# Layer norm and gate logits computed tile by tile inside the attention and neighbour loops

## The chip, the cores and the metric

The kernel runs on one core of one Trainium2 chip. The metric is the device time of one execution in microseconds (us), and for a kernel the median of its runs.

## What is computed

A graph network with a mixture of experts, in two layers: masked attention over 3327 nodes of 256 features, experts, a neighbour sum, experts again. Each stage takes the layer norm of the running x and adds its result to x. Cut from the reference:

```python
def _layernorm(x, axis=-1, eps=1e-05):
    m = jnp.mean(x, axis=axis, keepdims=True)
    v = jnp.var(x, axis=axis, keepdims=True)
    return (x - m) / jnp.sqrt(v + eps)
# attention (L0_gnn): h = x @ edge_w; e = where(adj > 0, h @ h.T, NEG_BIG)
#   output = adj * (node_att * softmax(e, axis=1)) @ (x @ weight) + bias
# experts (both ffn): logits = xt @ Wg + bg   (the second has no bias)
#   top_vals, top_idx = top_k(logits, 2); top_probs = softmax(top_vals)
#   y = sum over the 8 experts of gate * expert(xt)
# neighbours (L1_gnn): relu((adj @ x) @ W.T + b)
x = x + _L0_gnn_ref(_layernorm(x), adj, ...)
x = x + _L0_ffn_ref(_layernorm(x)[None], L0_ffn_Wg, L0_ffn_bg, ...)[0]
x = x + _L1_gnn_ref(_layernorm(x), adj, L1_gnn_W, L1_gnn_b)
x = x + _L1_ffn_ref(_layernorm(x)[None], L1_ffn_gate_w, ...)[0]
```

The change concerns the second and the fourth layer norm, and the logits `xt @ Wg` that follow them.

## The kernel before

Rows of x are handled in 26 tiles of 128 (T = 26, the last with 127). The program is a series of stages with a barrier of all engines between them: `project`, `attend`, `route` and `experts` of layer 0, `combine`, `neighbours`, `route` and `experts` of layer 1, `combine`. Inside a stage each engine runs its own instruction list in order, with waits on semaphores; nothing reorders them. `tiles` (L42) unrolls the first two and the last two tiles of a loop and runs the rest two at a time, with two buffer slots.

- **attend.** GpSimd copies the tile's h (L399) and turns its adjacency row block into a mask (L401). TensorE computes the scores of tile t+1 in 7 chunks (L502), then multiplies the probabilities of tile t in 7 groups of up to 4 blocks (L537, L539). VectorE masks the scores of t+1 (L444), forms the low parts of the transposed probabilities group by group (`rest`, L429), and then writes x_out (L471 to L478) and its row sums (`bn_stats`, L482). SP loads the adjacency (L371) and x, and stores x_out (L359). The row sums of all tiles stay in one buffer, `ST`.
- **route.** VectorE turns `ST` into mean and 1/std for all tiles (L133 to L146, with the square root on ScalarE, L151), SP loads all of x again (L690), VectorE normalises it tile by tile (L791), TensorE transposes it (L733) and multiplies it by the gate weights (L747) with copies on ScalarE (L778), SP stores the normalised x to `xn` in DRAM (L697) for the experts' gathers, and loads the expert weights (L928, L929). From L813 on the routing chain follows, nearly all on VectorE: top two, softmax, places of the pairs.
- **neighbours.** For tile t TensorE transposes the stored mask in 4 groups (L1326), ScalarE (L1384) and VectorE (`odd`, L1417) widen them, TensorE multiplies by the normalised x (L1333). The tail of tile t-1 stands inside tile t: `add` on VectorE (L1423), two transposes (L1342), the product with W (L1348), and `finish` on VectorE: pre (L1427), x_out (L1433), row sums (L1436). GpSimd makes two identities and then has nothing to do. SP loads the mask two tiles ahead (L1298), stores x_out (L1293) and loads x (L1301).

VectorE's step of the neighbour loop, before:

```python
def step(t, uses, slot, first, last):
    very_first = first and slot == 0
    if not very_first:
        add(t - 1, 1 - slot, first)
    odd(t, slot, 1, first)
    odd(t, slot, 3, first)
    if not very_first:
        finish(t - 1, uses - (1 - slot), 1 - slot, first)
```

## Time and profile before

| | |
|---|---|
| median of 3 runs | 1936.64 us (1935.55 to 1937.98) |
| span of the profiled execution | 1937.9 us, 1.3 us above the median |
| TensorE busy | 1616.8 us (83%) |
| VectorE busy | 995.0 us (51%) |
| ScalarE busy | 663.5 us (34%) |
| GpSimd busy | 480.1 us (25%) |

The stages begin at about 88 us (attention), 652 (gate 0), 734 (experts 0), 1066 (combine), 1127 (neighbours), 1368 (gate 1), 1448 (experts 1) and 1892 (last combine). In the profile PE is TensorE's matmuls, PEld its weight loads, DVE VectorE, ACT ScalarE, POOL GpSimd, SP the queue that issues most transfers; a q behind the name is the engine's queue of DMA issues. The text behind `<-` at the end of a row is what ended the idle time before it.

### The profile page before, as it was taken

Reading aid. Unit: us, or ns where it says so; the run is one execution under the profiler, and the core shown is the slowest. Engines: PE = TensorE matmul, PEld = TensorE weight load, DVE = VectorE, ACT = ScalarE, POOL = GpSimd, SP = SyncE. Lnnn points to the kernel's source line nnn. Section 1 sums busy time; section 2 is a strip of 40 time slices with the busy share of each in tenths; the row PEclk is TensorE's granted clock in tenths of the full one; section 3 lists DMA queues with packets and bytes.
Section 4 is the critical chain, followed back from the end, with each engine's and each line's share of the span. In section 5 each row is a group of like instructions: output and inputs, shape, how many; then the busy total and the mean of one; then the engine's idle time right before and its main releaser. Section 6 shows DMA issues by size and latency. Waiting matters only on the chain. (4 is left out here: it accounts for less than half of the span.)

```text
span 1937.9 us, 34014 instructions
## 1 busy us (share of the span) xinstructions
PE 1616.8 (83%) x9896; PEld 1358.5 (70%) x9896; DVE 995.0 (51%) x2459; ACT 663.5 (34%) x1395; POOL 480.1 (25%) x812
## 2 busy tenths in 40 slices
PE   5899999999999647999998059999729999999990
PEld 4788888888888635778777035555617888888880
DVE  5455555555555464555553632323385556566543
ACT  2323333333333202223222523333204454554554
POOL 0021121121111004555554000000013454544530
PEclk9999999999999757999999579999559999999995
DMA  4033433433432551111111824333751111111118
GB/s 152 8 112 137 154 116 132 149 126 116 146 145 81 191 234 33 46 50 50 49 49 43 282 90 138 122 131 120 292 227 31 35 38 35 36 36 37 36 32 284
DMA packets 84823, 209.45 MB, mean 108 GB/s; under 512 B 8880, under 2 KB 66225, under 8 KB 80561
## 3 DMA queue, kind: packets, MB, share of 16 engines
q1 hardware_dynamic: 68176, 154.95, 23.0%
q0 software_dynamic: 11328, 30.95, 5.1%
q10 hardware_dynamic: 5280, 23.09, 3.0%
q8 instruction: 17, 0.28, 0.1%
q14 instruction: 22, 0.18, 0.0%
HBM read 150.89 MB, written 58.07 MB: 108 GB/s over the span
## 5 line engine op out<-in xcount | busy, mean ns | idle before, releaser
L1062 PE MATMUL bank<-ffn_w_in_parts,ffn_x_t 128*128 128x512 f32 x1416 | 363.6, 404 | 18.9 <-DVE ffn_w_in_parts L1189 18.8
L1062 PEld LDWEIGHTS bank<-ffn_w_in_parts,ffn_x_t 128*128 128x128 f32 x1416 | 259.4, 191 | 78.6 <-DVE ffn_w_in_parts L1189 28.1
L1086 PE MATMUL bank<-ffn_w_out_parts,ffn_hidden_t 128*128 128x256 f32 x2124 | 286.0, 289 | 25.8 <-DVE ffn_hidden_t L1178 25.7
L1086 PEld LDWEIGHTS bank<-ffn_w_out_parts,ffn_hidden_t 128*128 128x128 f32 x2124 | 264.5, 193 | 30.3 <-issue 20.0
L502 PE MATMUL bank<-h_t,attn_h_tile 128*128 128x512 f32 (+1 forms) x1092 | 250.7, 385 | 10.5 <-POOL attn_h_tile L399 6.8
L537 PE MATMUL bank<-support,attn_probs_t 128*128 128x512 f32 x650 | 245.4, 411 | 1.1 <-DVE attn_probs_t L429 1.1
L502 PEld LDWEIGHTS bank<-h_t,attn_h_tile 128*128 128x128 f32 x1092 | 199.3, 192 | 51.9 <-POOL attn_identity L389 7.0
L417 ACT CAST attn_probs_t<-bank 128x512 fp32r<-128x512 f32 (+1 forms) x182 | 98.8, 558 | 350.0 <-PE bank L511 350.0
L1128 ACT ACTIVATE ffn_silu_or_gelu<-bank,w_b_in 128x128 f32<-128x128 f32 x472 | 134.2, 367 | 190.6 <-PE bank L1073 190.6
L429 DVE TENSOR_TENSOR attn_probs_t<-bank,attn_probs_t 128x512 fp32r<-128x512 f32 (+1 forms) x182 | 116.5, 652 | 161.4 <-ACT attn_probs_t L417 161.4
L539 PE MATMUL bank<-support,attn_probs_t 128*128 128x256 f32 x676 | 185.6, 281 | 0.0
L1333 PE MATMUL bank<-normed_parts,nbr_adj_t 128*128 128x512 f16 x676 | 165.1, 383 | 7.7 <-ACT nbr_adj_t L1384 7.7
L444 DVE CUSTOM_DVE_ANT_0 attn_scores<-bank,attn_mask 128x512 f32<-128x512 f32 (+1 forms) x182 | 116.5, 648 | 66.4 <-issue 66.4
L1178 DVE TENSOR_TENSOR ffn_hidden_t<-ffn_silu_or_gelu,ffn_hidden_t 128x512 fp32r<-128x512 f32 x118 | 80.5, 692 | 133.4 <-ACT ffn_hidden_t L1134 133.4
L537 PEld LDWEIGHTS bank<-support,attn_probs_t 128*128 128x128 f32 x650 | 122.3, 188 | 23.5 <-issue 1.3
L1025 POOL DMA_INDIRECT y<-ffn_y,ffn_dst x118 | 122.5, 1038 | 56.1 <-issue 55.9
L1014 POOL DMA_INDIRECT ffn_x_gathered<-xn,ffn_tok x118 | 126.9, 1075 | 20.5 <-issue 5.3
L539 PEld LDWEIGHTS bank<-support,attn_probs_t 128*128 128x128 f32 x676 | 127.6, 189 | 1.1
L399 POOL CAST attn_h_tile<-h_t 128x512 fp32r (+1 forms) x26 | 15.9, 611 | 416.2 <-DMA adj_tile<-in_adj 416.1
L1326 PE MATMUL bank<-nbr_identity,nbr_mask 128*128 128x128 bf16 x676 | 56.0, 222 | 73.5 <-DMA nbr_mask<-mask 71.9
L1326 PEld LDWEIGHTS bank<-nbr_identity,nbr_mask 128*128 128x128 bf16 x676 | 47.4, 99 | 90.5 <-issue 72.6
L1333 PEld LDWEIGHTS bank<-normed_parts,nbr_adj_t 128*128 128x128 f16 x676 | 61.4, 99 | 68.4 <-ACT nbr_adj_t L1384 12.0
(233 smaller groups left out, 2221.9 us busy)
## 6 DMA issues: line engine op xcount, KB each, us to landing
adj_tile<-in_adj SPq DMA_DIRECT2D x25, 1663.5 KB, 8.5
mask<-attn_mask ACTq DMA_DIRECT2D x26, 832.0 KB, 3.4
nbr_mask<-mask SPq DMA_DIRECT2D x26, 832.0 KB, 4.4
comb_y<-y SPq DMA_DIRECT2D x12, 768.0 KB, 10.4
w_w_in<-in_w SPq DMA_DIRECT2D x2, 4096.0 KB, 17.7
w_w_in<-in_w_t SPq DMA_DIRECT2D x2, 4096.0 KB, 17.4
x_normed<-x SPq DMA_DIRECT2D x6, 768.0 KB, 7.1
xn<-x_normed SPq DMA_DIRECT2D x6, 768.0 KB, 35.3
```

The lines of the kernel that those rows point to most:

```text
L429: dve.tensor_tensor(PT[:, half(slot, g), 1, 0:gn * P], bank[4 + half(slot, g)][:, 0:gn * P], PT[:, half(slot, g), 0, 0:gn * P].bitcast(F32 ...
L444: dve.tensor_tensor_reduce(out=SC[:, slot, c0:c0 + cn], in0=bank[c % 4][:, 0:cn], in1=NEG[:, slot, c0:c0 + cn], scale=1.0, scalar=-3.0e38, ...
L502: ins = pe.matmul(bank[c % 4][:, 0:cn], HS[:, slot, hs, k, :], HT[:, hm, k, c0:c0 + cn], start=n == 0 and k == 0, stop=n == 2 and k == KD - 1)
L537: pe.matmul(bank[6 + slot][:, :], part[:, 0, :], SUP[:, jt, :, :].rearrange("p a d -> p (a d)"), start=jt == 0, stop=False)
L539: ins = pe.matmul(bank[6 + slot][:, 0:D], part[:, 1, :], SUP[:, jt, 0, :], start=False, stop=False)
L1014: pool.indirect_dma_start(out=XG[:, slot, :], out_offset=None, in_=a["xn"], in_offset=bass.IndirectOffsetOnAxis(ap=TOKS[:, slot:slot + 1], ...
L1025: pool.indirect_dma_start(out=a["y"], out_offset=bass.IndirectOffsetOnAxis(ap=DSTS[:, slot:slot + 1], axis=0), in_=YS[:, slot, :], in_offs ...
L1062: ins = pe.matmul(bank[2 + 2 * slot + b][:, :], XT[:, slot, xp, k, :], WIP[:, wp, k, b * CH:(b + 1) * CH], start=n == 0 and k == 0, stop=n ...
L1086: ins = pe.matmul(bank[7][:, 0:D], HTT[:, hp, k, :], WOP[:, wp, k, :], start=n == 0 and k == 0, stop=n == 2 and k == KH - 1)
L1128: ins = act.activation(GATE[:, j, k * P:(k + 1) * P], src[:, k * P:(k + 1) * P], ACT.Gelu, bias=w.BI[:, bass.ds(e * KH + (4 * j + k), 1)])
L1326: ins = pe.transpose(bf[g % 2][:, j * P:(j + 1) * P], NEG[:, slot, (g0 + j) * P:(g0 + j + 1) * P], ID[:])
L1333: ins = pe.matmul(bank[2 + slot][:, :], AT[:, g % 2, j * P:(j + 1) * P], XH[:, g0 + j, :, :].rearrange("p a d -> p (a d)"), start=g0 + j = ...
```

## The change

A class `Gate` does layer norm and logits of one row tile inside the loop that produces the tile. VectorE aggregates the tile's own row sums (`stats`), GpSimd computes 1/std by a power and one Newton step in 8 dependent operations of one column, normalises the tile into `XN`, and multiplies it by all 8 gate vectors at once (`norm`, a product of 128 x 2048); SP stores `XN`; VectorE sums the products in four pieces of two experts (`reduce`) and adds the bias (`logits`). In attention GpSimd runs `norm(t - 3)` at the head of its step t, and VectorE sums tile t-1 between the groups of tile t. In the neighbour loop GpSimd runs `norm` alone, and VectorE sums tile t-2 in step t. At the start of each loop stage GpSimd waits for the gate weights, broadcast to 128 partitions, and reorders them.

The gate stages keep only the routing chain. The weights of layer 0 are loaded at the start of gate 0; `w_in` of layer 1 is loaded in step 3 of the neighbour loop's SP queue, `w_out` and the biases in gate 1.

```diff
+class Gate:
+    NORM_STEPS = 8
+    PIECES = 4
...
+    def load(self, act):
+        flat = self.gate_w.rearrange("p k e -> (p k e)")
+        act.dma_start(self.PR[:].rearrange("p e d -> p (e d)"), flat.partition_broadcast(P)).then_inc(self.w_loaded, 16)
...
+    def prepare(self, pool):
...
+        pool.wait_ge(self.w_loaded, 16 if self.gate_b is None else 32)
+        raw = self.PR[:].rearrange("p e d -> p (e d)").rearrange("p (q k e) -> p e k q", k=KD, e=E)
+        for k in range(KD):
+            pool.tensor_copy(self.GW[:, :, k * P:(k + 1) * P], raw[:, :, k, :]).then_inc(self.w_ready, 1)
+        pool.wait_ge(self.w_ready, self.n_ready())
...
+    def stats(self, dve, t, slot):
+        dve.bn_stats(self.ROW[:, slot, :], self.XO[:, slot, :]).then_inc(self.sums_ready, 1)
+        dve.wait_ge(self.sums_ready, t + 1)
+        if not known(t) or t >= 2:
+            dve.wait_ge(self.normed, t - 1)
+        dve.memset(self.TAKER[:], 0.0)
+        dve.bn_aggr(self.MV[:, slot, :], self.ROW[:, slot, :]).then_inc(self.stats_ready, 1)
+
+    def norm(self, pool, t, uses, slot):
+        def link(ins):
+            ins.then_inc(self.norm_step, 1)
+            link.n += 1
+            pool.wait_ge(self.norm_step, t * self.NORM_STEPS + link.n)
...
+        pool.wait_ge(self.stats_ready, t + 1)
+        link(pool.tensor_tensor(v, var, eps, ALU.add))
+        link(pool.tensor_tensor(minus, mean, minus_one, ALU.mult))
+        link(pool.tensor_tensor(r, v, minus_half, ALU.pow))
+        link(pool.tensor_tensor(tmp, r, r, ALU.mult))
+        link(pool.tensor_tensor(tmp, tmp, v, ALU.mult))
+        link(pool.tensor_tensor(tmp, tmp, minus_half, ALU.mult))
+        link(pool.tensor_tensor(tmp, tmp, three_halves, ALU.add))
+        link(pool.tensor_tensor(r, r, tmp, ALU.mult))
+        if not known(t) or t >= 2:
+            pool.wait_ge(self.xn_stored[slot], uses * 16)
+        pool.tensor_tensor(self.POOL_TAKER[:], eps, eps, ALU.add)
+        pool.tensor_scalar(self.XN[:, slot, :], self.XO[:, slot, :], minus, r, ALU.add, ALU.mult).then_inc(self.normed, 1)
+        pool.wait_ge(self.normed, t + 1)
+        if not known(t) or t >= 1:
+            pool.wait_ge(self.reduced, t * self.PIECES)
+        pool.tensor_tensor(self.PR[:], self.XN[:, slot, :].unsqueeze(1).to_broadcast([P, E, D]), self.GW[:],
+                           ALU.mult).then_inc(self.product_ready, 1)
+
+    def store(self, sp, t, slot):
+        sp.wait_ge(self.normed, t + 1)
+        sp.dma_start(self.xn[bass.ds(t * P, P), :], self.XN[:, slot, :]).then_inc(self.xn_stored[slot], 16)
+
+    def reduce(self, dve, t, slot, piece):
+        n = E // self.PIECES
+        dve.wait_ge(self.product_ready, t + 1)
+        dve.tensor_reduce(out=self.LS[:, slot, piece * n:(piece + 1) * n], in_=self.PR[:, piece * n:(piece + 1) * n, :],
+                          axis=AX, op=ALU.add).then_inc(self.reduced, 1)
+
+    def logits(self, dve, t, slot):
...
+        dve.wait_ge(self.reduced, (t + 1) * self.PIECES)
+        dve.tensor_tensor(self.LG[:, t, :], self.LS[:, slot, :], self.GB[:], ALU.add).then_inc(self.logits_ready, 1)
...
@@ attend, gpsimd
                 def step(t, uses, slot, first, last):
+                    if not known(t) or t >= 3:
+                        gate.norm(pool, t - 3, uses - 2 + slot, 1 - slot)
                     if not first:
                         pool.wait_ge(adj_in[slot], uses * 16 + (16 if last else 0))
...
                 pool.wait_ge(edge, 1)
-                tiles(pool, T, step)
+                gate.prepare(pool)
+                tiles(pool, T, step, head=6)
+                for t in range(T - 3, T):
+                    gate.norm(pool, t, t // 2, t % 2)
@@ attend, vector
-                    rest(t, slot, range(EARLY, NG))
+                    for g in range(EARLY, NG):
+                        rest(t, slot, [g])
+                        if g - EARLY < Gate.PIECES and not (first and slot == 0):
+                            gate.reduce(dve, t - 1, 1 - slot, g - EARLY)
+                    if not (first and slot == 0):
+                        gate.logits(dve, t - 1, 1 - slot)
...
-                    dve.bn_stats(a["ST"][:, t, :], XO[:, slot, :]).then_inc(sums_ready, 1)
+                    gate.stats(dve, t, slot)
...
+                for piece in range(Gate.PIECES):
+                    gate.reduce(dve, T - 1, (T - 1) % 2, piece)
+                gate.logits(dve, T - 1, (T - 1) % 2)
@@ route, sync
-                for sem, (lo, hi) in zip(x_loaded, spans):
-                    sp.dma_start(X[:, lo:hi, :], view[:, lo:hi, :]).then_inc(sem, 16)
-
-                sp.wait_ge(x_loaded[-1], 16)
-                w.load(sp)
...
-                    sp.dma_start(out[:, lo:hi, :], X[:, lo:hi, :]).then_inc(xn_stored, 16)
-                sp.wait_ge(xn_stored, len(spans) * 16)
+                load(sp)
...
@@ neighbours, sync
                     sp.dma_start(NEG[:, slot, :], a["mask"][t, :, :]).then_inc(mask_in[slot], 16)
+                    if not known(t) or t >= 3:
+                        gate.store(sp, t - 3, 1 - slot)
                     if not first:
                         store(t - 2, slot)
                     sp.dma_start(XB[:, slot, :], a["x2"][bass.ds(t * P, P), :]).then_inc(x_loaded[slot], 16)
-                tiles(sp, T, step)
...
+                    if known(t) and t == 3:
+                        w.load_in(sp)
+                tiles(sp, T, step, head=4)
@@ neighbours, gpsimd
+                gate.prepare(pool)
+                tiles(pool, T, lambda t, uses, slot, first, last: gate.norm(pool, t, uses, slot))
@@ neighbours, vector
-                    dve.bn_stats(a["ST"][:, t, :], XO[:, slot, :]).then_inc(sums_ready, 1)
+                    gate.stats(dve, t, slot)
...
                     odd(t, slot, 1, first)
+                    if not first:
+                        for piece in range(Gate.PIECES // 2):
+                            gate.reduce(dve, t - 2, slot, piece)
                     odd(t, slot, 3, first)
+                    if not first:
+                        for piece in range(Gate.PIECES // 2, Gate.PIECES):
+                            gate.reduce(dve, t - 2, slot, piece)
+                        gate.logits(dve, t - 2, slot)
                     if not very_first:
                         finish(t - 1, uses - (1 - slot), 1 - slot, first)
...
                 tiles(dve, T, step)
+                for t in (T - 2, T - 1):
+                    for piece in range(Gate.PIECES):
+                        gate.reduce(dve, t, t % 2, piece)
+                    gate.logits(dve, t, t % 2)
```

The transposes and the 8-column matmuls of `route`, its square root and its normalisation leave the program; the normalised x of all tiles is no longer kept in SBUF.

Where the moved work stands on VectorE in the neighbour loop is the point on which most depends. One tile of its list (an unrolled one, t = 24), before; `nbr_sum` is `add`, `nbr_adj_t` is `odd` for groups 1 and 3, the last three rows are `finish` of tile 23:

```order
L1423 TENSOR_TENSOR nbr_sum<-bank,nbr_sum_hi 128x256
L1417 TENSOR_SCALAR nbr_adj_t<-bank 128x1024
L1417 TENSOR_SCALAR nbr_adj_t<-bank 128x256
L1427 TENSOR_TENSOR nbr_before_relu<-bank,nbr_bias 128x256
L1433 SCALAR_TENSOR_TENSOR nbr_x_out<-nbr_before_relu,nbr_x 128x256
L1436 BN_STATS row_sums<-nbr_x_out 128x6
```

The same tile of VectorE's list in the changed kernel, where the sums are those of tile 22 and the statistics those of tile 23:

```order
L1489 TENSOR_TENSOR nbr_sum<-bank,nbr_sum_hi 128x256
L1483 TENSOR_SCALAR nbr_adj_t<-bank 128x1024
L240 TENSOR_REDUCE nbr_logit_sums<-nbr_gate_products 128x2 x2
L1483 TENSOR_SCALAR nbr_adj_t<-bank 128x256
L240 TENSOR_REDUCE nbr_logit_sums<-nbr_gate_products 128x2 x2
L247 TENSOR_TENSOR logits<-nbr_logit_sums,nbr_gate_b 128x8
L1493 TENSOR_TENSOR nbr_before_relu<-bank,nbr_bias 128x256
L1499 SCALAR_TENSOR_TENSOR nbr_x_out<-nbr_before_relu,nbr_x 128x256
L198 BN_STATS nbr_row_sums<-nbr_x_out 128x6
L202 MEMSET nbr_dve_wait_taker 128x1
L203 BN_AGGR nbr_mean_var<-nbr_row_sums 128x2
```

Four sums and the logits of the tile before stand ahead of `finish`, two of them ahead of the second widening.

GpSimd's list at the start of the attention stage, in the changed kernel:

```order
L492 MEMSET attn_identity 128x128
L494 AFFINE_SELECT attn_identity<-attn_identity 128x128
L496 MEMSET adj_tile 128x2
L184 MEMSET attn_constants 128x1 x4
L190 COPY attn_gate_w<-attn_gate_products 128x8x128 x2
L505 CAST attn_h_tile<-h_t 128x512
L507 ISA
L507 TENSOR_SCALAR attn_mask<-adj_tile 128x3328
```

The constants and the two reordering copies are new there, and stand ahead of the first tile's copy and mask.

## Rows read from the trace of the kernel before

**Rows 1.** Windows: two stages; busy us (instructions) by engine, clock, DMA share, GB/s
```profile
core 0: us, PE busy (x) PEld busy (x) DVE busy (x) ACT busy (x) POOL busy (x), PEclk, DMA share, GB/s
88.00:652.00 564.00, 552.71 (x3120) 478.56 (x3120) 295.39 (x962) 181.10 (x234) 93.30 (x55) 0.99 0.35 124
...
1127.00:1368.00 241.00, 221.03 (x1508) 132.13 (x1508) 67.33 (x156) 69.85 (x104) 0.93 (x4) 0.96 0.37 122
```
**Rows 2.** Timeline, gate 0: start, us, engine, line, operation [idle before, releaser]
```profile
651.96 4.06 SPq L690 DMA_DIRECT2D x_normed<-x  x4
...
654.20 0.13 POOL L724 IOTA gate_pair_low<- 128x1 f32 x1
...
693.49 0.37 DVE L813 TENSOR_REDUCE gate_top<-gate_logits 128x26 f32<-128x208 f32 x1
```
**Rows 3.** Timeline, gate 1: its start and the chain's first reduction
```profile
1368.14 3.70 SPq L690 DMA_DIRECT2D x_normed<-x  x4
...
1407.21 0.37 DVE L813 TENSOR_REDUCE gate_top<-gate_logits 128x26 f32<-128x208 f32 x1
```
**Rows 4.** DMA issues, 652 to 735 us: KB each, median us to landing
```profile
w_w_out<-in_w SPq DMA_DIRECT2D x1, 4096.0 KB, 33.3
...
xn<-x_normed SPq DMA_DIRECT2D x3, 768.0 KB, 34.5
```
**Rows 5.** Timeline, experts 0, GpSimd: two dependent operations of one column
```profile
803.85 0.20 POOL L1010 COPY ffn_tok<-route_tok 128x1 int32 x1
804.13 0.19 POOL L1013 TENSOR_TENSOR ffn_wait_taker<-ffn_identity 128x1 f32<-128x1 f32 x1
```
**Rows 6.** Groups by shape, GpSimd: the mask; busy us, mean ns
```profile
L401 POOL TENSOR_SCALAR attn_mask<-adj_tile 128x3328 bf16<-128x3328 f32 x26 | 77.1, 2964 | 9.3 <-issue 7.3
```
**Rows 7.** Timeline, attention, about one tile: VectorE and GpSimd
```profile
318.65 0.43 DVE L482 BATCH_NORM_STATS2 row_sums<-attn_x_out 128x256 f32 x1
...
326.77 0.61 POOL L399 CAST attn_h_tile<-h_t 128x512 fp32r x1 [17.15 <-DMA adj_tile<-in_adj]
...
329.85 0.69 DVE L429 TENSOR_TENSOR attn_probs_t<-bank,attn_probs_t 128x512 fp32r<-128x512 f32 x1 [1.58 <-ACT attn_probs_t L417]
331.69 0.69 DVE L429 TENSOR_TENSOR attn_probs_t<-bank,attn_probs_t 128x512 fp32r<-128x512 f32 x1 [1.15 <-ACT attn_probs_t L417]
```
**Rows 8.** Timeline, gate 0, VectorE: a sum over 472 elements
```profile
704.72 0.65 DVE L860 TENSOR_REDUCE gate_value<-gate_expert_cmp 128x59 f32<-128x472 f32 x1
```
**Rows 9.** Timeline, attention start: the first mask, and who waits for it
```profile
96.31 2.96 POOL L401 TENSOR_SCALAR attn_mask<-adj_tile 128x3328 bf16<-128x3328 f32 x1 [7.32 <-issue]
...
99.39 0.06 DVE L443 MEMSET attn_wait_taker<- 128x1 f32 x1 [12.84 <-POOL attn_mask L401]
...
100.19 4.21 PE L502 MATMUL bank<-h_t,attn_h_tile 128*128 128x512 f32 x9 [3.65 <-DVE attn_max L444]
```
**Rows 10.** DMA issues: a small broadcast and a large load, us to landing
```profile
adj_tile<-in_adj SPq DMA_DIRECT2D x25, 1663.5 KB, 8.5
...
attn_bias<-in_bias SPq DMA_DIRECT2D x1, 128.0 KB, 3.3
```
**Rows 11.** Timeline, attention end: the last tile's statistics
```profile
649.19 0.43 DVE L482 BATCH_NORM_STATS2 row_sums<-attn_x_out 128x6 f32<-128x256 f32 x1
```
**Rows 12.** Timeline, neighbour loop, one tile of VectorE
```profile
1342.49 0.42 DVE L1427 TENSOR_TENSOR nbr_before_relu<-bank,nbr_bias 128x256 f32<-128x256 f32 x1 [2.30 <-PE bank L1348]
...
1343.62 0.43 DVE L1436 BATCH_NORM_STATS2 row_sums<-nbr_x_out 128x256 f32 x1
...
1348.53 0.29 DVE L1417 TENSOR_SCALAR nbr_adj_t<-bank 128x256 f16<-128x256 bf16 x1 [3.25 <-PE bank L1326]
...
1351.05 0.42 DVE L1427 TENSOR_TENSOR nbr_before_relu<-bank,nbr_bias 128x256 f32<-128x256 f32 x1 [2.23 <-PE bank L1348]
```
**Rows 13.** Timeline, neighbour end: the last but one tile's statistics
```profile
1360.62 0.43 DVE L1436 BATCH_NORM_STATS2 row_sums<-nbr_x_out 128x6 f32<-128x256 f32 x1
```
**Rows 14.** Windows, attention start, behind TensorE's wait: columns as in rows 1
```profile
100.20:104.20 4.00, 4.00 (x9) 3.13 (x10) 2.49 (x11) 0.00 (x0) 2.78 (x1) 0.50 1.04 366
```

More of the change, by code:

```diff
@@ L39, with tiles @@
 PAIR_ROWS = 2 * NP
-def tiles(eng, count, step):
+def tiles(eng, count, step, head=2):
     turns = (count - 2) // 2
-    step(0, 0, 0, True, False)
-    step(1, 0, 1, True, False)
-    with eng.Fori(1, turns) as i:
+    for t in range(head):
+        step(t, t // 2, t % 2, t < 2, False)
+    with eng.Fori(head // 2, turns) as i:
         step(i * 2, i, 0, False, False)
@@ L1301, in step @@
                     sp.dma_start(XB[:, slot, :], a["x2"][bass.ds(t * P, P), :]).then_inc(x_loaded[slot], 16)
-                tiles(sp, T, step)
-                store(T - 2, 0)
-                store(T - 1, 1)
+                    if known(t) and t == 3:
+                        w.load_in(sp)
+                tiles(sp, T, step, head=4)
+                gate.store(sp, T - 3, (T - 3) % 2)
+                for t in (T - 2, T - 1):
+                    store(t, t % 2)
+                    gate.store(sp, t, t % 2)
+                gate.end(sp)
                 for slot in range(2):
@@ L1376, in _ @@
                 act.dma_start(BB[:], a["b"].partition_broadcast(P)).then_inc(w_loaded, 16)
+                gate.load(act)
                 def even(t, slot, g, first):
```

172 lines of the change are left out of this document (78 added, 94 removed).

## The prediction

> **What bounds the kernel now.** I read the stages first, by windows. In the attention stage TensorE is busy 552.7 of 564 us, in the neighbour stage 221.0 of 241 us [rows 1]: both loops run at TensorE's pace, VectorE is half busy or less, and GpSimd does nearly nothing in the neighbour stage (0.93 us). Then the timeline of the two gate stages. Gate 0 starts at 651.96 and the first reduction of its routing chain at 693.49 [rows 2]; gate 1 starts at 1368.14 and its chain at 1407.21 [rows 3]. That head, 41.5 and 39.1 us, is normalising, transposing and multiplying all 26 tiles, and nothing else runs beside it but transfers. It is what the change moves into the loops. So the question is whether the loops carry it for nothing. I took one tile of each loop and asked when the moved work can begin, and who waits for its result.
>
> **The heads go: -76.5 us.** What stays ahead of the chain is GpSimd's constants: its last one begins at 654.20 and takes 0.13 us, 2.4 us into the stage [rows 2]; without the two identity instructions it ends some 2.0 us in. So gate 0 gains 41.5 - 2.0 = 39.5 and gate 1 39.1 - 2.1 = 37.0. The weights of layer 0 are now loaded at the start of gate 0, beside a chain of 42 us: 12 MB landed within 34 us of their issue [rows 4], so I cost this at nothing; if that load were slower by 10 us, the experts would wait for it.
>
> **GpSimd's price for one tile, L.** L runs from the end of VectorE's row statistics to the finished product. Eight dependent 128x1 operations come first, each waiting for the one before: such a pair stands 0.28 us apart [rows 5], so 8 x 0.28 = 2.25. Then the wait taker 0.19, and the norm of 256 elements. The one-input rate of GpSimd is (2.96 - 0.19) / 3328 = 0.83 ns an element [rows 5, 6], so 0.19 + 0.21 = 0.40. Then a wait, 0.12, and the product: 2048 elements of two inputs. No row shows a large two-input operation on GpSimd. Bounds from the mask row: one pass over the elements, 0.19 + 1.7 = 1.9; two reads and a write with no overlap, three passes, 5.3. I take two and a half passes, 4.45, since an engine that needs a full pass for one input will hardly take the second free, and some of the write may overlap. With 0.2 for the two hand-overs between engines, **L = 7.6 us** (5.05 to 8.5). The power operation could cost more than 0.28; no row shows it, and I allow 1 us on top for it.
>
> The Trainium skill (GPSIMD Engine Reference, section 3.1) speaks against putting this product here: it gives 4497 ns for a GpSimd add of two fp32 inputs of 2048 elements, about twice VectorE. By that figure the sum below would be the same; by the one-pass price it would be 69 us lower. No trace so far shows which holds.
>
> **Attention loop: 0.** A tile takes 21.1 us. Statistics end at 319.1 [rows 7]; with the new aggregate (0.3, an estimate from VectorE's small operations of 0.15 to 0.2) L ends at 327.0. The first sum stands behind the group's subtraction that starts at 329.85, so after 330.5: 3.5 us to spare. A sum reads 512 elements, 0.65 x 512 / 472 = 0.70 us [rows 8], and stands in a gap of 1.15 us that VectorE has before each subtraction. GpSimd's next tile copy waits for the adjacency until 326.77, so the norm ahead of it delays the mask by 0.2 us, and TensorE wants that tile some eight us later. SP's one more store needs a norm of a tile before. If L passed 11 us, VectorE would wait here, and behind it TensorE.
>
> **Attention start: +9.5.** GpSimd now waits for the gate weights and reorders them before its first tile copy and mask. VectorE's first score waits for that mask (12.84 us), and TensorE in turn for VectorE [rows 9]; the 7.32 us before the mask stay. A broadcast of 1 MB lies between 3.3 us (128 KB) and 8.5 us (1.66 MB) to landing [rows 10]; in proportion 6.3, of which 5.8 fall after GpSimd is ready. Two copies of 1024 strided elements: 1.0 each by the one-pass rate, 2.6 by three passes; I take the middle, 3.7 for both. 5.8 + 3.7 = 9.5 (7.9 to 11).
>
> The Trainium skill (GPSIMD Engine Reference, section 7) gives about 2.9 cycles an element for reads with a step over 8 bytes, as here; by it the copies would take 5 us and the start would cost 10.8.
>
> **Attention end: +10.** The last tile has nothing to hide behind: the statistics end at 649.6 [rows 11], then 0.3 + L + four sums at 0.73 + 0.3 for the logits = 11.1, so 660.7; the stage change, 2.35 us before because of the last store, will take 1 to 2.35. 662 or so against 651.96 [rows 2].
>
> **Neighbour loop: +108.** Here the order decides. VectorE's step t sums the products of tile t-2, but the statistics of t-2 end the step before. So each tile runs through a ring that nothing shortens: statistics end, L on GpSimd (7.6), two sums (1.45), the second widening of the transposed mask (0.32), two sums (1.45), logits with their wait (0.3), then pre, x_out and statistics, 1342.49 to 1344.05 = 1.56 [rows 12], and the aggregate (0.35). Together 13.05 us. Now a tile takes 1351.05 - 1342.49 = 8.56 us [rows 12]. The tile's add and first widening fit into VectorE's wait. TensorE waits for the second widening, which is queued behind the sums, and idles 4.5 us a tile. The step runs 24 times with sums: 24 x 4.5 = 108.
>
> **Neighbour end: +12.5.** From the statistics of the last but one tile: L, its sums 2.9 and logits 0.3; GpSimd's second product waits for these sums and runs from about 10.8 to 15.3, then sums and logits 3.3, and 1.0 to the next stage, 19.6. Before it was 1368.14 - 1361.05 = 7.1 [rows 3, 13].
>
> **Neighbour start and weight load: +2 and +8.** One more MB at the start adds 3 us or less before TensorE's weights are in; 2. The 8 MB of w_in are issued in SP's step 3, ahead of the mask of tile 4. A transfer behind weights waited its turn: stores issued behind them took 34.5 us [rows 4]. At 12 MB in 34 us the 8 MB take 23, the mask needs 2 more, and TensorE wants it about one and a quarter new tiles (16 us) later: 25 - 16 = 9, I take 8 (0 to 14).
>
> **Sum.** -76.5 + 0 + 9.5 + 10 + 108 + 12.5 + 2 + 8 = +73.5. The profiled execution's span is 1937.9, 1.3 above the median 1936.64; so 1936.6 + 73.5 = **2010 us**. One us in L is worth 24 in the loop and 3 at the ends, 27. With L = 5.05 the sum is +4 (1941), with 8.5 it is +98 (2034), with a slow power +100. A measurement of this kernel can tell 0.2% (4 us) from no change.
>
> **Rivals.**
> (a) *Faster, because GpSimd is quick.* The ring decides only by L. The total turns to a gain below L = 7.6 - 73.5/27 = 4.9. It takes a product of one pass and the small operations back to back at 0.19 (1.5 instead of 2.25): L = 4.3, so 1936.6 + 73.5 - 27 x 3.3 = 1921. For it: the mask row, whose rate is one element a cycle. Against it: two inputs. Chance 0.06, and 0.02 that it lands within 0.2% of no change.
> (b) *TensorE's clock falls in the neighbour loop.* TensorE now waits twice a tile, 4.5 us together. In the attention start a wait of 3.65 us was followed by 4 us at a granted 0.50, the level of 1.2 GHz [rows 14]. If the longer wait of each tile does the same, some 4 us of TensorE's 8.4 run twice as long; most fits into its idle time, I put 1 to 2 us a tile on the ring: 2034 to 2058. Against it: that wait should stay near 3 us. Chance 0.12.
> (c) *The attention loop is not covered.* Were L over 11, or a sum over 1.15 us beside GpSimd's reads, VectorE's subtractions would come late; with 1 us for each of 25 tiles, and the same L in the ring, over 2060. Chance 0.05.
> (d) *The change does its part without the ring*: if the products were ready at once, as with L below 3.1, all but the ends would be gained, near 1895. The order of VectorE's rows excludes it nearly; its chance is in (a).
> The forecast's case has 0.75. Chances: faster 0.06, same 0.02, slower 0.92. The range for 8 in 10: 1965 (a product of two passes or less, and half of the weight stall) to 2050 (three passes with a slower power, or the clock).
>
> **What the next profile would show.** Right: a neighbour tile of about 13 us with VectorE idle before its first sum, released by GpSimd's product; the product near 4.5 us; gate stages of about 44 us; attention tiles still 21.1 us; one long TensorE wait for a mask near the fourth neighbour tile. Wrong: a product under 2.5 us, neighbour tiles under 10 us, or attention tiles over 21.5.

## The result, and the profile after

| | median us | runs | against the kernel before |
|---|---|---|---|
| before, same chip | 1936.64 (1935.55 to 1937.98) | 3 | |
| changed | 2000.81 (2000.06 to 2003.6) | 4 | 1.0333 (95%: 1.0318 to 1.0347) |

One run of the kernel before (2500.36 us) and one of attention_only (2032.79 us) fell in a slower state of the chip and are in no median here.

The change costs 64.2 us, 3.3%; forecast were +73.5 and 2010. The profiled execution has a span of 1998.5 us, 60.6 more than the profiled execution before. I split these 60.6 us by the first instruction of each stage. The timeline of the changed kernel, GpSimd's and VectorE's rows at the two ends of loops and at the experts' starts (start, us, engine, line, operation [idle before, releaser]):

```profile
656.29 0.43 DVE L198 BATCH_NORM_STATS2 attn_row_sums<-attn_x_out 128x6 f32<-128x256 f32 x1
...
668.57 0.20 POOL L797 MEMSET gate_before<- 128x128 bf16 x1 [3.71 <-POOLq L101]
670.37 0.37 DVE L855 TENSOR_REDUCE gate_top<-logits 128x26 f32<-128x208 f32 x1 [2.75 <-POOL gate_pair_low L813]
...
711.02 0.30 POOL L1057 MEMSET ffn_zero<- 1x256 f32 x1 [40.68 <-POOLq L101]
...
1465.23 0.20 POOL L797 MEMSET gate_before<- 128x128 bf16 x1 [3.99 <-POOLq L101]
...
1507.67 0.30 POOL L1057 MEMSET ffn_zero<- 1x256 f32 x1 [40.67 <-POOLq L101]
```

Gate 0 now takes 711.02 - 668.57 = 42.45 us, where it took 82.2 (651.96 to 734.16); its chain begins 1.8 us into the stage, [rows 2] had 41.5. Gate 1 takes 42.44, where it took 79.74. So the two stages give back 39.75 + 37.3 = 77.05 us. The neighbour stage before them began at 1126.99 and now begins at 1102.21; it ended at 1368.14 [rows 3] and now ends at 1465.23: 241.15 us have become 363.0. That is +121.9, nearly all of what is lost. The rest: attention start +5.0, its loop and last tile +2.1, its end +9.5, everything else -0.9. Sum: -77.05 + 121.9 + 5.0 + 2.1 + 9.5 - 0.9 = +60.6.

One turn of the neighbour loop, from the same timeline, answers to [rows 12]:

```profile
1250.57 1.28 DVE L240 TENSOR_REDUCE nbr_logit_sums<-nbr_gate_products 128x2 f32<-128x512 f32 x2 [6.83 <-POOL nbr_gate_products L230]
1251.76 0.28 DVE L1483 TENSOR_SCALAR nbr_adj_t<-bank 128x256 f16<-128x256 bf16 x1
1251.96 1.27 DVE L240 TENSOR_REDUCE nbr_logit_sums<-nbr_gate_products 128x2 f32<-128x512 f32 x2
...
1252.10 0.60 PE L1398 MATMUL bank<-normed_parts,nbr_adj_t 128*128 128x512 f16 x2 [3.04 <-DVE nbr_adj_t L1483]
...
1252.99 3.29 PE L1398 MATMUL bank<-normed_parts,nbr_adj_t 128*128 128x512 f16 x8
1253.37 0.17 DVE L247 TENSOR_TENSOR logits<-nbr_logit_sums,nbr_gate_b 128x8 f32 x1
1253.46 0.42 DVE L1493 TENSOR_TENSOR nbr_before_relu<-bank,nbr_bias 128x256 f32<-128x256 f32 x1
...
1254.01 0.43 DVE L1499 SCALAR_TENSOR_TENSOR nbr_x_out<-nbr_before_relu,nbr_x 128x256 f32<-128x256 f32 x1
...
1254.47 0.43 DVE L198 BATCH_NORM_STATS2 nbr_row_sums<-nbr_x_out 128x6 f32<-128x256 f32 x1
...
1254.94 0.18 DVE L203 BATCH_NORM_AGGREGATE nbr_mean_var<-nbr_row_sums 128x2 f32<-128x6 f32 x1
...
1255.19 0.19 POOL L215 TENSOR_TENSOR nbr_rstd<-nbr_mean_var,nbr_constants 128x1 f32<-128x1 f32 x1 [4.66 <-DVE nbr_mean_var L203]
...
1255.74 0.55 POOL L217 TENSOR_TENSOR nbr_rstd<-nbr_rstd,nbr_constants 128x1 f32<-128x1 f32 x1
...
1257.89 0.56 POOL L226 TENSOR_SCALAR nbr_x_normed<-nbr_x_out,nbr_rstd 128x256 f32<-128x256 f32 x1
...
1258.62 4.51 POOL L230 TENSOR_TENSOR nbr_gate_products<-nbr_x_normed,nbr_gate_w 128x2048 f32<-128x2048 f32 x1 [0.17 <-POOL nbr_x_normed L226]
...
1263.16 1.28 DVE L240 TENSOR_REDUCE nbr_logit_sums<-nbr_gate_products 128x2 f32<-128x512 f32 x2 [7.04 <-POOL nbr_gate_products L230]
```

Follow the brackets: VectorE waits 7.04 us for GpSimd's product, GpSimd waited 4.66 us for VectorE's statistics. Neither is busy all the time (between 1200 and 1400 us GpSimd works 112.1 of 200 us and VectorE 83.4), and each waits for the other once a tile: a ring of 1263.16 - 1250.57 = 12.59 us, where a tile took 8.56 to 8.64. TensorE waits too (3.04 us), for the widened mask that stands between VectorE's sums. The groups of the changed kernel (busy us, mean ns, idle before by releaser) say the same for the whole loop:

```profile
L240 DVE TENSOR_REDUCE nbr_logit_sums<-nbr_gate_products 128x2 f32<-128x512 f32 x104 | 66.0, 678 | 164.8 <-POOL nbr_gate_products L230 164.8
L230 POOL TENSOR_TENSOR nbr_gate_products<-nbr_x_normed,nbr_gate_w 128x2048 f32<-128x2048 f32 x26 | 117.2, 4508 | 4.0 <-POOL nbr_x_normed L226 3.6
```

### The profile page after: what moved, and what is told of

Same layout as the page of the kernel before. It is cut to its first block and busy times, and to the rows that moved or that the text cites. A ratio compares the mean times of both kernels' runs of the same rounds, so it can differ in the third digit from the quotient of the medians.

```text
span 1998.5 us, 34639 instructions
## 1 busy us (share of the span) xinstructions
PE 1578.9 (79%) x9584; PEld 1302.8 (65%) x9584; DVE 1112.2 (56%) x2745; ACT 648.0 (32%) x1365; POOL 862.5 (43%) x1392
## 5 line engine op out<-in xcount | busy, mean ns | idle before, releaser
L1398 PE MATMUL bank<-normed_parts,nbr_adj_t 128*128 128x512 f16 x676 | 185.4, 418 | 68.2 <-DVE nbr_adj_t L1483 67.4
L1398 PEld LDWEIGHTS bank<-normed_parts,nbr_adj_t 128*128 128x128 f16 x676 | 65.8, 106 | 141.1 <-DVE nbr_adj_t L1483 72.9
L240 DVE TENSOR_REDUCE nbr_logit_sums<-nbr_gate_products 128x2 f32<-128x512 f32 x104 | 66.0, 678 | 164.8 <-POOL nbr_gate_products L230 164.8
L1080 POOL TENSOR_TENSOR ffn_wait_taker<-ffn_identity 128x1 f32<-128x1 f32 x118 | 22.7, 192 | 300.1 <-DVE ffn_y L1282 189.2
L1070 POOL DMA_INDIRECT ffn_x_gathered<-xn,ffn_tok x118 | 127.2, 1078 | 20.4 <-issue 6.8
L1391 PE MATMUL bank<-nbr_identity,nbr_mask 128*128 128x128 bf16 x676 | 61.7, 236 | 91.3 <-DMA nbr_mask<-mask 89.1
```

The costliest lines, as they stand in the source:

```text
L1070: pool.indirect_dma_start(out=XG[:, slot, :], out_offset=None, in_=a["xn"], in_offset=bass.IndirectOffsetOnAxis(ap=TOKS[:, slot:slot + 1], ...
L1398: ins = pe.matmul(bank[2 + slot][:, :], AT[:, g % 2, j * P:(j + 1) * P], XH[:, g0 + j, :, :].rearrange("p a d -> p (a d)"), start=g0 + j = ...
```

## Experiments

The theory at the start is that of the prediction, the **ring**: a tile of the neighbour loop costs the latency from statistics to product (L) plus VectorE's steps behind it. The rivals change from run to run and stand in the expectations. The kernel before has medians of 1936.2 to 1940.9 us beside these runs; every ratio is against it on the same chip. Differences in us between two changed kernels compare medians that mostly come from different chips, on which the kernel before itself differs by up to 4.6 us; the traces say more of them.

### Shorter latency: no_newton

```diff
-    NORM_STEPS = 8
+    NORM_STEPS = 3
-        link(pool.tensor_tensor(tmp, r, r, ALU.mult))
...
-        link(pool.tensor_tensor(r, r, tmp, ALU.mult))
```

This leaves out the Newton step that refines 1/std on GpSimd.

> Edit: the five operations of the Newton step on 1/std are left out in both loops (the power alone gives 1/std), so L is 5 x 0.27 = 1.35 us shorter. The Newton step's part of the computation is left out. Ring theory: each of 23 tiles is 1.35 us shorter and three times more at the ends (attention end once, neighbour end twice): 31 + 4 = 35 us less, 1966 us; attention tiles unchanged at 21.05. If the ring does not set the pace: under 5 us less.

1963.38 us (1962.18 to 1965.6), ratio 1.0132 (1.0108 to 1.0155): 37.4 us less than the change. The spacing of the statistics fell from 12.6 to 11.3 us. Five operations of 0.27 us make 1.35 us. From the first statistics of the loop to the last the trace has 292.51 us, where the change has 323.06: 25 spacings of 1.35 less are 34, and the one stall in the loop is 3.3 longer. The ends and the last attention tile give 4.4 more. The loop goes by latency: in the change GpSimd idles 44% of it, and five of its operations of one column still cost their full length in every tile.

### The order of VectorE's steps: sums_behind

```diff
                     odd(t, slot, 1, first)
-                    if not first:
-                        for piece in range(Gate.PIECES // 2):
-                            gate.reduce(dve, t - 2, slot, piece)
                     odd(t, slot, 3, first)
                     if not first:
-                        for piece in range(Gate.PIECES // 2, Gate.PIECES):
+                        for piece in range(Gate.PIECES):
                             gate.reduce(dve, t - 2, slot, piece)
```

> Edit: in the neighbour loop all four sums and the logits stand behind the second widening of the mask (odd, group 3), so that TensorE's last multiply of a tile no longer waits for GpSimd. If the ring through GpSimd and VectorE sets the pace, TensorE's wait only moves to another place: the tile stays 12.6 us, 2000 us within 3. If TensorE's wait of 2.6 to 3.8 us for the widening (and the clock that falls behind it) is what costs, the tile falls by 2.5 to 4 us: 1910 to 1940 us.

1997.35 us (1991.95 to 1997.83), ratio 1.0297 (1.027 to 1.0323). TensorE no longer waits behind the sums for its mask, and the spacing fell only from 12.6 to 12.4 us, which is what the widening took in the ring: from the first sum to the logits it is 2.61 us for 2.80. TensorE's wait has moved, as the ring theory had it: it now waits for the first widening of the next tile, 1.73 and 3.88 us in turn (at 1256.61 and 1269.30), 41.6 us in the 200 us from 1200 on, where the change has 49.5. So its wait in the changed kernel is a symptom. The granted clock over these 200 us is 0.91 in both kernels, so this run says nothing of what the clock alone would cost.

### The stall behind the weights: w_in_late

```diff
-                    if known(t) and t == 3:
-                        w.load_in(sp)
...
-            route(nc, bank, "gate1", LG, r, w, w.load_out)
+            route(nc, bank, "gate1", LG, r, w, w.load)
```

> Edit: w_in of layer 1 is not loaded in the neighbour loop but at the start of gate 1, ahead of w_out. The 8 MB stood ahead of a mask: TensorE waited 17.9 us, and the step that had it took 23.9 instead of 12.6 us. Without it that step takes 12.6: 11.3 us less. In gate 1 17 MB at 12 MB in 34 us take 48 us beside a chain of 42: w_in (23 us) is in time, w_out and the biases come at 48 us against a use some 50 us in; so 1989 to 1992 us. If the load is no cause of that wait, 2000; if the transfers in gate 1 come late, up to 2000 as well, with VectorE waiting for w_out at the start of the experts.

1989.13 us (1984.36 to 1991.66), ratio 1.0256 (1.0229 to 1.0284), 11.7 us less than the change by the medians. The row that goes away is this one, TensorE's wait in the timeline of the changed kernel, for a mask issued at 1144.43 behind the w_in load of 1143.12:

```profile
1143.12 0.92 SPq L982 DMA_DIRECT2D w_w_in<-in_w_t  x2
1144.43 0.35 SPq L1354 DMA_DIRECT2D nbr_mask<-mask  x1
...
1167.30 0.93 PE L1391 MATMUL bank<-nbr_identity,nbr_mask 128*128 128x128 bf16 x7 [17.86 <-DMA nbr_mask<-mask]
```

One spacing of statistics was 23.87 us in the change, 12.6 with its neighbours; with w_in in gate 1 all are 12.5 to 12.7. The experts hardly pay for it, if at all: gate 1 takes 42.45 us, as with the early load; from there to the end of the program it is 492.1 us for 490.8, in a spread of 490.0 to 493.7 over the twelve profiled executions, and the trace has no wait of an engine for a weight.

### Opening the ring: lag3

```diff
-                            gate.reduce(dve, t - 2, slot, piece)
+                            gate.reduce(dve, t - 3, 1 - slot, piece)
...
-                tiles(dve, T, step)
-                for t in (T - 2, T - 1):
+                tiles(dve, T, step, head=4)
+                for t in (T - 3, T - 2, T - 1):
```

VectorE sums the products one tile later, so the product has a whole step to be made in.

> Edit: in the neighbour loop VectorE sums the products of tile t-3 in step t, not t-2; nothing else moves. If the ring (statistics, GpSimd 8.0 us, sums, finish: 12.63 us a tile against 8.63 before) is what the loop pays, it is cut here and a tile falls to what GpSimd alone needs, 8.0 to 9 us: 23 x 3.8 = 87 us less, about 1914 us. If work on VectorE or the sums ahead of TensorE's second widening were the cost, the tile stays near 12.6 us and the time near 2000. Third theory: the product now runs beside x_out (L1499, two SBUF inputs), which took 4.00 us instead of 0.42 in the one place where it met a product (last tile); then each x_out shows up to 4 us, the tile comes to 10 to 11 us, 1945 to 1960 us.

1983.25 us (1978.96 to 1985.25), ratio 1.0225 (1.0201 to 1.025). None of the three theories met it: 17.6 us less than the change, where the ring alone asked for 1914. The third, that the product would hold x_out up, came nearest, with the wrong instruction. The spacing is 11.0 to 12.7 us and irregular. The timeline of lag3 shows a new long row:

```profile
1256.17 4.51 POOL L230 TENSOR_TENSOR nbr_gate_products<-nbr_x_normed,nbr_gate_w 128x2048 f32<-128x2048 f32 x1 [1.58 <-DVE nbr_logit_sums L240]
1256.23 4.47 DVE L247 TENSOR_TENSOR logits<-nbr_logit_sums,nbr_gate_b 128x8 f32 x1
1260.63 0.41 DVE L1493 TENSOR_TENSOR nbr_before_relu<-bank,nbr_bias 128x256 f32<-128x256 f32 x1
1261.17 0.42 DVE L1499 SCALAR_TENSOR_TENSOR nbr_x_out<-nbr_before_relu,nbr_x 128x256 f32<-128x256 f32 x1
```

An addition of eight elements takes 4.47 us. It starts with GpSimd's product and ends with it. So it is in 22 of the 26 tiles, 20 of them in the group below (the expectation of the next run counts only these); the same line in the attention loop takes 0.16:

```profile
L247 DVE TENSOR_TENSOR logits<-nbr_logit_sums,nbr_gate_b 128x8 f32 x20 | 89.4, 4471 | 3.1 <-DVE nbr_logit_sums L240 1.9
...
L247 DVE TENSOR_TENSOR logits<-attn_logit_sums,attn_gate_b 128x8 f32 x22 | 3.4, 157 | 0.0
```

The sums' end releases the product (one buffer of products), and the addition is VectorE's next instruction. So the order that opened the ring put the two side by side in each tile. The Trainium skill (SBUF — State Buffer, "Who interferes with whom") says that the two engines share one pair of SBUF ports under an exclusive lock, that a VectorE instruction with two inputs in SBUF contends for it with a GpSimd instruction that reads SBUF, and that the order of issue decides which of the two blocks. The rows agree: the addition starts 0.06 us behind the product and takes 4.47 us beside its 4.51. The next three runs test it.

### The lock, one instruction at a time: logits_late, no_lock

logits_late is lag3 with the addition between the two halves of the next step's sums:

```diff
+                    if not known(t) or t >= 4:
+                        gate.logits(dve, t - 4, slot)
                     odd(t, slot, 3, first)
...
                             gate.reduce(dve, t - 3, 1 - slot, piece)
-                        gate.logits(dve, t - 3, 1 - slot)
```

> Edit: lag3 (sums of tile t-3 in step t), and the addition of the gate's bias to the sums (L247) moved from the end of the step to between the two halves of the next step's sums, where no product runs. In lag3 the trace shows what kept its loop at 11.03 us and more a tile: the addition L247, 0.16 us long elsewhere, takes 4.47 us in 20 of the 26 tiles, and it starts with the product of POOL and ends with it; all of VectorE's later work, x_out (L1499) first, stands behind it. Lock theory (a VectorE instruction with two inputs in SBUF doesn't run beside a POOL instruction that reads SBUF): with the addition out of the way the next instruction with two inputs in SBUF is x_out itself, which then starts when the product ends; the ring is product 4.50, then x_out to the next product's start 6.03 (1250.14 to 1256.17 in lag3), so 10.53 a tile; mean spacing 10.5 to 10.7 where lag3 has 11.2: 1983 - 25 x 0.6 = 1968 (1962 to 1975), and x_out is the long instruction (mean 2 us or more instead of 0.55). Rival, the addition alone was slow (its 128x8 form, or a semaphore): x_out stays 0.42, the spacing falls to the 8.64 us of the kernel before, and the time to 1911 to 1920. Rival, VectorE's or POOL's total work sets the spacing: nothing changes, 1983.

1958.44 us (1956.87 to 1961.19), ratio 1.0088 (1.0071 to 1.0105). The addition is back at 0.16 us, and the blocked instruction is now x_out, in the timeline of logits_late:

```profile
1332.27 4.51 POOL L230 TENSOR_TENSOR nbr_gate_products<-nbr_x_normed,nbr_gate_w 128x2048 f32<-128x2048 f32 x1 [1.58 <-DVE nbr_logit_sums L240]
1333.30 0.42 DVE L1493 TENSOR_TENSOR nbr_before_relu<-bank,nbr_bias 128x256 f32<-128x256 f32 x1 [1.11 <-PE bank L1413]
1333.86 3.20 DVE L1499 SCALAR_TENSOR_TENSOR nbr_x_out<-nbr_before_relu,nbr_x 128x256 f32<-128x256 f32 x1
```

L1493, with one input in PSUM, runs in 0.42 us in the middle of the product; L1499, with both in SBUF, ends at 1337.06, 0.28 after the product. Its mean over 26 tiles is 2918 ns. The spacing is 10.35 to 10.68 but for the first tiles and the stall. The time is 10 us below my figure: I had reckoned lag3's mean spacing as 11.2 us, and behind the stall it was 11.6, so that a tile gained 1.0 us (298.94 us from the first statistics to the last, now 274.12) for 0.6.

no_lock is logits_late, and the value before the ReLU goes to the free half of its PSUM bank:

```diff
-                    dve.tensor_tensor(PRE[:, slot, :], bank[6 + slot][:, 0:D], BB[:], ALU.add)
+                    dve.tensor_tensor(bank[6 + slot][:, D:2 * D], bank[6 + slot][:, 0:D], BB[:], ALU.add)
...
-                    dve.scalar_tensor_tensor(XO[:, slot, :], PRE[:, slot, :], 0.0, XB[:, slot, :], ALU.max, ALU.add)
+                    dve.scalar_tensor_tensor(XO[:, slot, :], bank[6 + slot][:, D:2 * D], 0.0, XB[:, slot, :], ALU.max, ALU.add)
```

> Edit: logits_late, and in addition the value before the ReLU (PRE) is written to the free second half of its PSUM bank instead of to SBUF, so that x_out (L1499) has one input in SBUF and one in PSUM. Lock theory: nothing of VectorE that can meet a product has two inputs in SBUF any more; the product of 4.50 us runs beside the steps, the ring is gone and the neighbour loop has the spacing of the kernel before, 8.64 us (211.9 us from the first statistic to the last, 299 in lag3, of which some 15 are the wait for the mask behind the weights): 1983 - 72 = 1911 (1905 to 1922). The work theory (POOL has 8.2 us a tile of norm and product, with no slack for its waits) would leave about 9.2 us a tile: 1925. If reading PSUM doesn't take it out of the lock: as logits_late, 1968.

1916.16 us (1914.29 to 1918.73), ratio 0.9878 (0.9861 to 0.9894): 1.2% faster than the kernel before. In its timeline x_out takes 0.42 us beside the product, and the next turn comes 8.64 us later:

```profile
1327.17 4.52 POOL L230 TENSOR_TENSOR nbr_gate_products<-nbr_x_normed,nbr_gate_w 128x2048 f32<-128x2048 f32 x1 [0.82 <-DVE nbr_logit_sums L240]
...
1335.81 4.53 POOL L230 TENSOR_TENSOR nbr_gate_products<-nbr_x_normed,nbr_gate_w 128x2048 f32<-128x2048 f32 x1 [0.90 <-DVE nbr_logit_sums L240]
1336.84 0.43 DVE L1493 TENSOR_TENSOR bank<-bank,nbr_bias 128x256 f32<-128x256 f32 x1 [1.11 <-PE bank L1413]
1337.40 0.42 DVE L1499 SCALAR_TENSOR_TENSOR nbr_x_out<-bank,nbr_x 128x256 f32<-128x256 f32 x1
```

The statistics stand 8.63 or 8.64 us apart, as before the change; only the wait behind w_in remains (one spacing of 29.03). GpSimd is busy 83.07 of 100 us between 1250 and 1350, TensorE 96.36 at a granted clock of 1.00. The work theory falls: the same work of GpSimd fits under TensorE's 8.64 us. The order has a price of its own at the end of the stage, where three tiles are left to sum and not two: 19.5 us behind the last statistics for 12.5, and the 1914 of lag3's ring theory had not counted it.

### The control: psum_alone

The PSUM edit alone, on the changed kernel, sums still those of tile t-2.

> Edit: the change, with the value before the ReLU in PSUM (x_out has one input in SBUF), everything else as in the change: the sums stay those of tile t-2. Ring theory: in the change itself the product starts only after x_out of the same tile, so the lock blocks nothing but the x_out of the last tile (4.00 us in its trace, 0.42 here), and there the two products behind each other set the end anyway; 12.6 us a tile as before, time 2000 (1995 to 2002, the same as the change). Rival, the lock is what made the change slow: the spacing falls to 8.64 us and the time to 1911 to 1920.

2000.95 us (1996.29 to 2003.5), ratio 1.0327 (1.0305 to 1.035): the same as the change. The lock is not what made the change slow. Its order of steps kept x_out ahead of the product; the ring had to be opened first, and only then did the lock cost anything. The one place where the change meets it is its last tile, where two x_out follow each other:

```profile
1447.88 4.50 POOL L230 TENSOR_TENSOR nbr_gate_products<-nbr_x_normed,nbr_gate_w 128x2048 f32<-128x2048 f32 x1
1448.66 4.00 DVE L1499 SCALAR_TENSOR_TENSOR nbr_x_out<-nbr_before_relu,nbr_x 128x256 f32<-128x256 f32 x1
```

### The two halves, and the start: attention_only, masks_first

attention_only has the attention loop and gate 0 of the change, `neighbours` and gate 1 as before.

> Edit: the attention loop and gate 0 as in the change; neighbours and gate 1 (normalisation, transposes, products on TensorE, x_out loaded again) as in the kernel before. By the two traces: gate 0 -39.75, attention start +5.0, attention loop +2.1, attention end +9.5, the rest -1.6; so 1936.2 - 24.7 = 1911.5 (1908 to 1916). If the attention half had other costs later (x normed in DRAM in tiles of 128 KB, the placement of memory), it would be above 1920.

1917.02 us (1914.7 to 1917.15), ratio 0.9872 (0.9852 to 0.9891): 1.3% faster, 24.8 us at this ratio, where the split of the two traces had 24.7. That they agree so closely is in part luck, since the interval is 21 to 29 us and the attention start of this kernel's profiled execution cost 2.5 us more than the change's (see the table in the section on the prediction). The median is 5.5 us over my number, and the kernel before on that chip (1940.85) 4.6 over the 1936.2 that I reckoned from. The attention half was a gain from the start; the neighbour half lost it more than three times over (+121.9 - 37.3 = 84.6 us).

masks_first moves GpSimd's preparation behind its first two masks:

```diff
                         ALU.mult, ALU.add).then_inc(mask_ready, 1)
+                    if known(t) and t == 1:
+                        gate.prepare(pool)
...
-                gate.prepare(pool)
                 tiles(pool, T, step, head=6)
```

> Edit: the change, with POOL's constants and the two copies of the gate's weights behind the masks of steps 0 and 1 instead of ahead of them. By the trace the two copies (3.73 us) and the landing of the weights ahead of them hold the first mask back; best_mix had its first statistic at 129.95 us where no_lock had it at 133.78: the time falls by 3.7 to 3.9 us, 1997 (1994 to 1999). Rival, the first mask is late for the transfer of the gate's weights alone (2 MB that stands in the queues ahead of adj): less than 1 us.

1993.29 us (1992.52 to 1995.17), ratio 1.0285 (1.0263 to 1.0307). That is 7.5 us under the change, twice my figure. The first statistics come 3.7 us sooner (130.28 us for 133.95), and the last ones of the attention stage 3.1 us sooner. Its neighbour stage starts 3.2 us sooner (1098.98 for 1102.22), and another 1.9 us lie between that and its first statistics (25.6 us for 27.4), where the edit changes nothing; over the twelve profiled executions that stretch is 25.2 to 27.7 us long, so they are spread. The attention start has a spread too: in the nine kernels that share the change's attention start, the first attention statistics stand 46.5 to 49.5 us behind the start of their stage, and the change's own (46.5) is among the earliest; here it is 42.2. So the edit is worth 4.3 us beside the change's profiled execution and up to 7.3 beside the others. Whether this makes up the 7.5 us of the medians no run shows, since only one execution of each kernel has a trace. The rival (under 1 us) falls in any case.

### A version that beats both: best_mix

no_lock with w_in in gate 1 and masks_first.

> Edit: no_lock, with w_in of layer 1 loaded in gate 1 (w_in_late) and the copies of the gate weights in attention moved behind POOL's masks of step 1. Lock theory: no_lock's 1911 less 11.7 (w_in_late) less 3.7 (two copies of 1.9 us that stood ahead of the first mask): 1896 (1888 to 1906). If the lock stays 1953; if the copies at their new place hold the next mask up, 1900.

1890.18 us (1889.44 to 1892.1), ratio 0.9738 (0.9722 to 0.9754): 2.6% under the kernel before, 5.5% under the change, and 26 us under no_lock where I had 15 (11.7 for the stall and 3.7 for the start, from 1911). Its statistics are 8.63 or 8.64 us apart, with no stall; the stall that w_in_late took away cost 12 us in a ring of 12.6 and 20.4 in no_lock (29.03 - 8.64), where the next masks are wanted sooner. With 3.8 from the start that is 24.2. Of that the traces show 22.2, the difference between the spans of the two profiled executions (1912.6 and 1890.4); the experts of layer 1 and the last combine take 2.1 us more here, within the spread of that stretch over all traces (490.0 to 493.7 us).

## Why the prediction was right

The mechanism was the one told, and five of the eight terms came within about 2 us. The largest was 12 us too high. The terms that were too high are 19 us off together and those too low 7, so the sum looks a little better than its parts: +60.6 in the traces for +73.5.

- **The heads go: -76.5.** Measured -77.05 (39.75 and 37.3).
- **L = 7.6.** Measured from the end of the aggregate (1255.12) to that of the product (1263.13): 8.0. The product took 4.51 us (forecast 4.45). No row had a price for it: two and a half passes were a choice between bounds of 1.9 and 5.3 us, each us of which is worth 27 in the sum, and that the choice came within 0.1 us is luck as far as the rows go. The Trainium skill (GPSIMD Engine Reference, section 3.1) has 4497 ns for an addition of this size. The trace agrees within 0.3% in the neighbour loop and within 3% in the attention loop (4.61 us). The power operation took 0.55 us, 0.36 more than the others (rows L215, L217), inside the 1 us that I had allowed; norm 0.56 for 0.40.
- **Neighbour loop: +108.** Mechanism and place as told: a ring, VectorE idle before its first sum, released by the product. Size: 12.6 for 13.05. In the turn shown the first sums and the widening take 1.39 us (forecast 1.77), the second sums 1.41 (1.45), the logits 0.09 (0.3), pre to statistics 1.44 (1.56), the aggregate 0.22 (0.35), and L with its hand-overs 8.04 (7.6): 12.59. A tile before was 8.64 and not 8.56. So a turn costs 4.0 us for 4.5. Counted as the prediction counts, to the statistics of the last but one tile, 207.10 us became 314.18: +107.1, of which 11.2 is the stall and 95.9 the ring, for 108. TensorE idles 48 of 200 us there, 3.0 a tile for the 4.5 forecast; the rest of the longer tile it works at a lower clock. no_newton and sums_behind confirm the ring by themselves. lag3 did not: it opened the ring and met the lock, and only no_lock, with both out of the way, has the spacing of the kernel before.
- **The weight stall: +8.** 11.2 in the trace, 11.7 by w_in_late.
- **Neighbour end +12.5 and start +2:** from the end of the last but one tile's statistics to gate 1 it was 7.09 us and is now 20.99 (1444.24 to 1465.23), +13.9; the start +0.9. The stage as a whole got +121.9 where the four terms said +130.5.
- **Attention start: +9.5.** For its size this term was off most: the first statistics came 5.0 us later (128.91, then 133.95). The two copies took 3.73 us as forecast (again the middle of two bounds). The 5 us estimated for them from the 2.9 cycles an element of the Trainium skill (GPSIMD Engine Reference, section 7) were too much. The wait for the weights was 4.3 for 5.8, and the first mask was late by 7.7 us. TensorE took that delay in full (it resumes at 107.94 for 100.19, 7.75 later), as I had assumed. What I missed is its clock. Its first 24 matmuls start 8.2 us later and take 8.43 us for 7.41, so its wait for the mask fell from 3.65 [rows 9] to 2.20 us, and in this execution the clock stays up behind it: 48 matmuls take 10.78 us, where the kernel before took 13.51, the first 4 us of them at a granted 0.50 [rows 14]. 7.75 - 2.73 = 5.0, the whole of what was measured. In the timeline and the windows of the changed kernel:

```profile
97.31 8.43 PE L621 MATMUL bank<-h_t,attn_h_tile 128*128 128x512 f32 x24 [15.16 <-POOL attn_h_tile L505]
107.94 10.78 PE L621 MATMUL bank<-h_t,attn_h_tile 128*128 128x512 f32 x48 [2.20 <-DVE attn_max L555]
```

```profile
107.90:111.90 4.00, 3.96 (x20) 3.39 (x21) 3.29 (x16) 0.00 (x0) 2.83 (x1) 1.00 0.96 299
```

  That the clock stayed up is not a property of the change. Nine kernels share this start, and their profiled executions differ (us; clock in the first 2 us or more behind the wait; the last column from the start of the stage to the first statistics):

  | kernel | wait | granted clock behind it | 48 matmuls | first statistics |
  |---|---|---|---|---|
  | logits_late, no_newton, changed, no_lock | 2.00, 2.07, 2.20, 2.35 | 1.00 | 10.75 to 10.78 | 46.5 to 46.6 |
  | psum_alone, lag3 | 2.56, 2.73 | 0.76 and 0.69, then 0.50 | 12.30, 12.28 | 48.0, 48.1 |
  | attention_only, sums_behind, w_in_late | 3.29, 3.48, 4.12 | 0.50 | 13.51, 13.43, 13.11 | 49.0, 49.2, 49.5 |
  | before | 3.65 | 0.50 | 13.51 | 41.3 |
  | masks_first, best_mix | 5.04, 5.11 | 0.50 | 12.91, 12.91 | 42.2, 42.3 |

  So the term is +5.2 to +8.2 us from one execution to another, counted from the start of the stage, and the prediction's 9.5 was 1.3 to 4.3 us too high; the +5.0 of the one trace is at its low end.

- **Attention loop: 0** and its **end: +10.** The statistics stay 21.03 to 21.10 us apart. The last tile takes 2.0 us more (17.02 for 15.01): it has no scores of a next tile, so VectorE comes to its first sum before the product is there, and the subtractions and TensorE wait behind it. The prediction had taken the 3.5 us to spare of a full tile for every tile. The end is +9.5 (2.77 us from statistics to gate 0, now 12.28).

```profile
647.95 0.69 DVE L240 TENSOR_REDUCE attn_logit_sums<-attn_gate_products 128x2 f32<-128x512 f32 x1 [1.49 <-POOL attn_gate_products L230]
```

- **Rival (b), the clock.** Its condition came true, though the wait stayed near 3 us, which the prediction had put against it; its price did not. Behind TensorE's wait of 3.04 us eight matmuls took 3.29 us, 1.89 elsewhere, at a granted clock of 0.55, near the 1.2 GHz level. In windows of the changed kernel, behind the wait and later in the same tile:

```profile
1253.00:1256.00 3.00, 3.00 (x11) 1.10 (x9) 2.65 (x9) 0.19 (x1) 0.65 (x3) 0.55 0.13 44
...
1256.80:1260.40 3.60, 3.60 (x23) 1.87 (x21) 0.00 (x0) 1.40 (x2) 3.12 (x7) 1.00 0.84 273
```

  But these matmuls are not in the ring: the steps of the turn listed above are all VectorE's and GpSimd's, with no idle time that TensorE ended, and they add up to the whole turn. So the clock cost the ring nothing, where I had put 1 to 2 us a tile.
- **Rivals (a), (c), (d)** needed L below 4.9, over 11, or below 3.1; L was 8.0.

What the prediction didn't see, and didn't need, is that the obvious cure of its ring would run into the lock. Whoever had costed "sum one tile later" from durations alone would have said 1914 and measured 1983.

## What to carry to other kernels

Work that fits under the bound engine by its sum (GpSimd 56% and VectorE 42% busy in the loop) still sets the pace if two engines wait for each other once a tile: write the ring down step by step, and ask which consumer can stand one tile later. Then look at what the new order puts side by side: a VectorE instruction with both inputs in SBUF, even of eight elements, can stand for the whole of a long GpSimd instruction; move it to where none runs, or give it an input in PSUM. And load weights where nothing with a deadline is queued behind them.

## What the runs showed of the hardware

- VectorE with two inputs in SBUF beside GpSimd's 4.5 us product: 4.47 us for a 128x8 addition that takes 0.16 alone, 3.20 and 4.00 us for an x_out that takes 0.42. VectorE instructions with at most one input in SBUF keep their time beside the same product (no_lock): L1493 0.43, x_out with its other input in PSUM 0.42, statistics 0.43, the widening of 1024 elements from PSUM 0.69.
- GpSimd: 4.51 us for 2048 products of two fp32 inputs in the neighbour loop and 4.61 in attention; 1.89 us for a copy of 1024 elements read with a step of 64 bytes; 0.55 us for a power of one column, 0.19 for an addition; 0.56 us for the norm of 256 elements.
- TensorE's clock: in the attention start waits of 2.00 to 2.35 us left it at a granted 1.00, and behind waits of 2.56 us and more it fell to 0.50, at once or within 2 us; 48 matmuls then took 12.3 to 13.5 us for 10.8. A wait of 3.04 us in the neighbour loop was followed by 0.55.
- Between GpSimd's tile copy (96.55) and the mask that follows it (104.05) lie 6.88 us that the profile puts down to issue; the kernel before has the same with 7.32 [rows 9], masks_first with 8.82. What it is stays open.
